# One tile's product of B and u divided between GpSimd and VectorE, and neighbouring products on GpSimd joined

## What is computed

```python
# x is normalised; then the state-space block, with d over 512 inner channels and n over 16 states
xs, res = split(rmsnorm(x) @ W_in)
xs = silu(conv4(xs) + conv_b)
dt, B, C = split(xs @ W_x)                 # 512, 16, 16
dt = softplus(dt @ W_dt)
h = exp(A * dt) * h + dt * B * xs          # for every d and n, step by step in time
y = sum_n(h * C)
out = x + (y * silu(res)) @ W_out          # and a residual around it
# the expert block: 8 chunks of 512 rows, each with weights of its own
h = silu(x @ w1[e]) * (x @ w3[e]);  x + h @ w2[e]
```

## Time and profile before

| | us |
|---|---|
| median of 3 runs (lowest, highest) | 978.1 (977.73, 979.46) |
| the profiled execution | 979.27 |
| its span | 977.5 |
| granted TensorE clock in it | 0.982 |

### The profile page before, as it was taken

How to read it: one execution, slowest core, us unless ns; L and a number is a source line. 1 busy time by engine, 2 the same in 40 slices (tenths; PEclk the granted TensorE clock), 3 DMA queues, 4 the chain that set the end, 5 groups by cost and what they waited for, 6 DMA issues and landing times. The chain is left out here.

```text
span 977.5 us, 13189 instructions
## 1 busy us (share of the span) xinstructions
PE 912.5 (93%) x4204; PEld 601.2 (62%) x4204; DVE 900.1 (92%) x1000; ACT 745.8 (76%) x1356; POOL 893.5 (91%) x425
## 2 busy tenths in 40 slices
PE   6989988999999999999999999999999998677988
PEld 4555455655766566755766567655667557554777
DVE  5889899899999999999999999999999989988983
ACT  4577877888779878888879787888788876567771
POOL 1498899999999999999999999999999999998970
PEclk9998999999999999999999999999999999699999
DMA  5580145011651039111471037310580117401100
GB/s 176 227 295 22 43 164 226 1 68 59 259 202 46 23 114 353 54 68 46 182 293 40 29 102 274 144 68 0 188 331 1 47 60 264 153 22 59 52 1 22
DMA packets 43477, 116.82 MB, mean 120 GB/s; under 512 B 8592, under 2 KB 27024, under 8 KB 34192
## 3 DMA queue, kind: packets, MB, share of 16 engines
q1 hardware_dynamic: 41552, 115.94, 31.9%
q10 hardware_dynamic: 1856, 0.04, 0.1%
HBM read 110.21 MB, written 5.77 MB: 119 GB/s over the span
## 5 line engine op out<-in xcount | busy, mean ns | idle before, releaser
L701 DVE TENSOR_TENSOR_SCAN ring<-ebank,state,ring 128x512 f32<-128x512 f32 (+1 forms) x544 | 626.4, 1203 | 36.8 <-ACT ebank L864 28.7
L553 POOL TENSOR_TENSOR hc<-ring,c_all 128x1024 f32<-128x1024 f32 (+1 forms) x256 | 600.4, 2367 | 18.4 <-DVE ring L701 10.7
L864 ACT ACTIVATE ebank<-dt_,a_neg 128x512 f32<-128x512 f32 (+1 forms) x544 | 353.0, 662 | 143.0 <-DVE ring L701 139.5
L1323 PEld LDWEIGHTS ybank<-ident,hc 128*128 128x128 f32 x1920 | 221.0, 142 | 95.4 <-issue 58.0
L542 POOL TENSOR_TENSOR ring<-b_all,u 128x1024 f32<-128x1024 f32 x110 | 261.1, 2374 | 9.9 <-DVE taken L644 9.5
L1323 PE MATMUL ybank<-ident,hc 128*128 128x128 f32 x1920 | 245.2, 276 | 23.0 <-POOL hc L553 14.3
L681 DVE TENSOR_TENSOR ring<-b_all,ubank 128x1024 f32<-128x1024 f32 x144 | 172.0, 1195 | 0.0
L1248 PE MATMUL gbank<-xT,w 128*128 128x512 f32 x280 | 132.0, 603 | 7.1 <-DVE hb L811 6.8
L1248 PE MATMUL gbank<-xT,w_a 128*128 128x512 f32 x256 | 120.1, 606 | 8.0 <-DVE dt_ L669 4.4
L1248 PE MATMUL gbank<-xs,w_a 128*128 128x512 f32 x224 | 100.8, 593 | 0.7 <-ACT sres L896 0.7
L1248 PEld LDWEIGHTS gbank<-xT,w 128*128 128x128 f32 x280 | 50.2, 192 | 64.0 <-issue 46.0
(11 more groups left out here) (164 smaller groups left out, 854.9 us busy)
## 6 DMA issues: line engine op xcount, KB each, us to landing
b_all<-bc_kept SPq DMA_DIRECT2D x32, 1024.0 KB, 6.7
c_all<-bc_kept SPq DMA_DIRECT2D x32, 1024.0 KB, 8.4
w<-in_L_ffn_w_dram SPq DMA_DIRECT2D x16, 640.0 KB, 4.9
w_a<-in_L_attn_W_in_dram SPq DMA_DIRECT2D x7, 1024.0 KB, 4.8
w_a<-wc_kept SPq DMA_DIRECT2D x7, 1024.0 KB, 4.9
w2s<-in_L_ffn_w_dram SPq DMA_DIRECT2D x8, 640.0 KB, 9.3
xin<-in_L_attn_x_dram SPq DMA_DIRECT2D x9, 512.0 KB, 3.8
x<-in_L_attn_x_dram SPq DMA_DIRECT2D x7, 512.0 KB, 6.4
```

Of the source, the lines that this page charges most:

```text
L553: ch_ok.by(e.tensor_tensor(tile_of(hc, c, q)[:, 0:many, :], tile_of(ring, c, q)[:, 0:many, :], c_all[:, n:n + many, tok], ALU.mult))
L701: h_ok.by(e.tensor_tensor_scan(row, e_of(c, j), row, initial=all_states[:, first:first + 1], op0=ALU.mult, op1=ALU.add))
L864: e_ok.by(e.activation(e_of(c, j), dt_[:, d, tok], ACT.Exp, scale=a_neg[:, d, n0 + n:n0 + n + 1]))
L1323: last = e.matmul(ybank[:, cols(b)], hc[:, q % HC, n, cols(b)], ident[:, :], is_transpose=True, start=(k == 0 and n == 0 and b == 0), stop ...
```

## The change

- `TWO`: in chunks 1 to 6 GpSimd makes the products of B and u for tiles 10 and 11, 17 and 18, 22 and 23 in one instruction each (`bu_two`, 2048 elements), at the place of the first of the two. It waits for what the second's slot needs as well.
- `SHARED`: in those chunks tile 21's product is divided. GpSimd makes state 0 at its old place, VectorE state 1 in a job after tile 20, behind `hidden(0)`, `hidden(1)` and `hidden_tail`. Before tile 21's scans VectorE waits for both.
- u is made for two blocks at once (`u_two`, 1024 elements): blocks 0 and 1 of the next chunk at tile 28, blocks 2 and 3 at tile 2 of the chunk itself. In chunk 0 only the pair at tile 28 is joined.
- On ScalarE `residual(0, 1)` at tile 5 becomes `residual(0)` at tile 4, ahead of `convolved(2)`, and `residual(1)` at tile 5, behind it.

```diff
+    SHARED = 21
+    TWO = (10, 17, 22)
     POOL_BU = (1, 4, 7, 10, 11, 14, 17, 18, 21, 22, 23, 24, 27, 29)
-    DVE_BU = tuple(q for q in range(Q) if q not in POOL_BU)
+    DVE_BU = tuple(q for q in range(Q) if q not in POOL_BU or q == SHARED)
...
         def wait_bu(e, c, q):
             if q in pool_bu(c):
                 bup_ok.wait(e, c, before(pool_bu(c), q) + 1)
-            else:
+            if q in dve_bu(c):
                 bud_ok.wait(e, c, before(dve_bu(c), q) + 1)
...
+        def steady(c):
+            return 0 < c < E - 1
...
+            def u_two(d):
+                def job(c, i):
+                    for k in (d, d + 1):
+                        wait_dt(e, c, k)
+                    xs_ok.wait(e, c)
+                    ub_ok.wait(e, c - 1, d + 2)
+                    e.tensor_tensor(u[:, d:d + 2, :], dt_[:, d:d + 2, :], xs[:, d:d + 2, :], ALU.mult).then_inc(u_ok.sem, 2)
+                return job
...
+                if steady(c) and q == SHARED:
+                    bup_ok.by(e.tensor_tensor(ring[:, q % RING, 0, :], b_all[:, n, :], u[:, d, :], ALU.mult))
+                    return
...
+            def bu_two(c, q):
+                d, n, many, tok = spot(c, q)
+                u_ok.wait(e, c, d + 1)
+                if d == 0:
+                    b_in[n // SG].wait(e, c)
+                    b_in[(n + NG) // SG].wait(e, c)
+                cb, qb = tile_before(c, q + 1, RING)
+                ch_ok.wait(e, cb, qb + 1)
+                st_ok.wait(e, cb, qb // 2 + 1)
+                dst = ring[:, q % RING:q % RING + 2, :, :].rearrange("p a n t -> p (a n) t")
+                e.tensor_tensor(dst, b_all[:, n:n + 2 * NG, :], u[:, d, :].unsqueeze(1).broadcast_to([P, 2 * NG, TC]), ALU.mult
+                                ).then_inc(bup_ok.sem, 2)
...
                 r = q + AHEAD
-                if r < Q and r in pool_bu(c):
+                if steady(c) and r in TWO:
+                    bu_two(c, r)
+                elif r < Q and r in pool_bu(c) and not (steady(c) and r - 1 in TWO):
                     bu(c, r)
...
-            table = [(4, "scan", u_of(ND - 1)), (10, "back", back), (21, "next", front), (24, "front", u_of(0)),
-                     (27, "front", u_of(1)), (29, "front", u_of(2))]
+            table = [(2, "scan", u_two(2)), (10, "back", back), (21, "next", front), (28, "front", u_two(0))]
...
+                if steady(c) and q == SHARED:
+                    bud_ok.by(e.tensor_tensor(ring[:, q % RING, 1, :], b_all[:, n + 1, :], ubank[:, :], ALU.mult))
+                    return
...
-                     (20, "back", hidden_tail), (21, "back", hidden(2)), (22, "back", hidden(3)), (23, "back", hidden(4)),
+                     (20, "back", hidden_tail), (20, "scan", bu_shared), (21, "back", hidden(2)), (22, "back", hidden(3)), (23, "back", hidden(4)),
...
-                     (3, "front", before_conv(3)), (3, "front", convolved(0)), (4, "front", convolved(1)), (5, "front", convolved(2)), (5, "back", residual(0, 1)),
+                     (3, "front", before_conv(3)), (3, "front", convolved(0)), (4, "front", convolved(1)), (4, "back", residual(0)), (5, "front", convolved(2)), (5, "back", residual(1)),
```

More of the change, by code:

```diff
@@ L569, in _ @@
                     bu(0, q)
-            table = [(4, "scan", u_of(ND - 1)), (10, "back", back), (21, "next", front), (24, "front", u_of(0)),
-                     (27, "front", u_of(1)), (29, "front", u_of(2))]
-            table0 = [(3, "late", u_of(1)), (7, "late", u_of(2)), (10, "late", u_of(3)), (23, "next", front),
-                      (27, "front", u_of(0)), (28, "front", u_of(1)), (29, "front", u_of(2))]
-            run(table, table0, [(4, "scan", u_of(ND - 1))], [], group)
+            table = [(2, "scan", u_two(2)), (10, "back", back), (21, "next", front), (28, "front", u_two(0))]
+            table0 = [(3, "late", u_of(1)), (7, "late", u_of(2)), (10, "late", u_of(3)), (23, "next", front), (28, "front", u_two(0))]
+            run(table, table0, [(2, "scan", u_two(2))], [], group)
         @block.vector
@@ L682, in bu, with bu_shared @@
                                           ub.unsqueeze(1).broadcast_to([P, many, tok.stop - tok.start]), ALU.mult))
+            def bu_shared(c, i):
+                if steady(c):
+                    bu(c, SHARED)
             def group(c, q):
@@ L705, in group @@
                     bu(c, q + 2)
-                elif q + 1 < Q and q + 1 in dve_bu(c) and (c, q) != (E - 1, QH + 1):
+                elif q + 1 < Q and q + 1 in dve_bu(c) and (c, q) != (E - 1, QH + 1) and not (steady(c) and q + 1 == SHARED):
                     bu(c, q + 1)
```

## The result

The change makes the kernel slower: 985.85 us (median of 4 runs, 985.32 to 986.53) against 978.06 before, a ratio of 1.0079 with a 95% interval of 1.0064 to 1.0093. Forecast were 983.7 and a range of 977.5 to 988.5. The profiled execution took 986.17, its span 984.4, that is 6.9 more than before. Lines have moved: the scans are L738 (L701 before), the products of c L583 (L553), single products of B and u L559 (L542), joined ones L572, the exponentials L901 (L864), the copies of state L910 (L873), the sum of y L1360 (L1323), the hidden products L848 (L811), the copy of the gate tail L1200 (L1163).

A forecast was written before the change was run, and what follows sets the result against it. The prediction took GpSimd and a ring through TensorE, ScalarE and VectorE to be tied. Six middle chunks x 0.97 = 5.8, less 0.2 in chunk 0, gave +5.6 on the median 978.1: 983.7 us, range 977.5 to 988.5.

The forecast's parts named there:

- The new wait: Joined product of tiles 17 and 18 waits for ScalarE's paired copy of tiles 14 and 15: GpSimd idle 1.9 us.
- the wait before tile 21: VectorE's wait for ScalarE before tile 21, 1.53 us in the kernel before, was to be 0.8 to 0.9.
- the 0.97 a chunk: Tile 17's scan starts 1.25 us later; after ScalarE's slack, silus and tile 21 follow and each middle chunk ends 0.97 later.
- the 0.28 of slack at tile 20: ScalarE's tail-copy wait absorbs part of tile 17's 1.25 us delay; tile 20's second exponential and the silus come 0.95 to 1.0 later.
- What GpSimd sheds: GpSimd's work per middle chunk falls 2.1 us: five joins save 5 x 0.20 = 1.0, half of tile 21 saves 1.09.
- the ring: Cycle through TensorE, ScalarE's tail copy and silus, VectorE's tile 21 and scans, ScalarE's y copy, TensorE; almost without GpSimd, tied with it.
- The residual's halves: First half ahead of ScalarE's third convolution copy removes VectorE's 0.70 us wait at tile 6; VectorE taken 0.75 earlier.
- GpSimd and the ring: GpSimd holds the cycle only before tile 12's sum, so its 2.1 us relief is worth at most some 0.15 a chunk.
- The paying rival: GpSimd was the bound: 2.1 x 6 = 12.6 us gained, 965.5 us, or 972 with half of it; chance 0.11.
- the stall: VectorE waits about 2.0 us at tile 17 for GpSimd's joined product; its scan starts 1.25 us later.
- The half tile on VectorE: VectorE's half of tile 21's product, 0.67 us, falls in its 1.53 wait for ScalarE: no cost, or 0.6 without that cover.
- The reason that the prediction gave: No port contention: scans take 1259 ns (median) both in the first 120 us, with GpSimd partly workless, and in the middle.

The follow-up runs named there:

- copy_alone: The change with all joins kept, but in chunks 1 to 6 ScalarE copies tile 14's last column by itself, a step earlier: 976.64 us, ratio 0.9981.
- join17_only: The kernel before plus only the join of tiles 17 and 18 in chunks 1 to 6: 989.14 us, ratio 1.0108.
- residual_whole: The change with the residual's four row blocks together again at tile 5, behind the third convolution's copy: 989.48 us, ratio 1.0114.
- residual_only: The kernel before plus only the residual's halves at tiles 4 and 5: 977.31 us, ratio 0.9985.
- no_joins: The change with no product of B and u and no u joined; tile 21's division and the residual's halves stay: 977.11 us, ratio 0.9980.
- no_join17: The change without the join of tiles 17 and 18 alone: 975.96 us, ratio 0.9979.
- tile21_whole: The change with tile 21's product whole on GpSimd: 984.49 us, ratio 1.0065.
- no_join17_y26: The change without the join of tiles 17 and 18, and with ScalarE's copy of y of block 2 at tile 26, not 27: 975.52 us, ratio 0.9971.
- the two last kernels: No joins of B and u, tiles 21 and 10 divided, residual's halves, y copy at tile 26: 974.24 us; the second also joins u at tile 28: 975.19.

## Why the prediction was right

- **The new wait**: right in kind and nearly in size. Forecast 1.9 us of idle time, measured 1.87; VectorE's wait "about 2.0", measured 1.99; the joined instruction 4.55, measured 4.54; the wait before tile 21 "0.8 to 0.9", measured 0.89. copy_alone and join17_only show that this alone is the cause. That the idle time came out so close is in part luck: GpSimd was done with tile 14 0.34 earlier than before (51.61 for 51.95 from the chunk's first scan) and not 0.6, which shortens it by 0.26, and the copy came and was taken up 0.21 later, which lengthens it.
- **The term that was mis-sized** is the 0.97 a chunk, which measured 1.17. Tile 17 was put 1.25 late and was 1.41. The residual's halves gave 0.66, not the 0.75 that I took, and GpSimd started 0.17 behind the copy's end, where 0.05 was taken. From there on the 0.28 of slack at tile 20 was as forecast (tile 19 was 1.44 late, tile 21 1.17). Six chunks x 1.17 = 7.0; chunk 0, from which 0.2 was taken off, is 0.09 shorter in the profile of the change; and the span grew by 6.9. The medians differ by 7.8, interval 6.3 to 9.1, where 5.6 was forecast.
- **What GpSimd sheds** was put too high: 2.1 a chunk, measured 1.75. The sum took means of single instructions, but one of GpSimd's instructions starts some 0.05 before the record of the last one ends. Back to back, starts in chunk 3 are 1.24 (512 elements), 2.32 (1024) and 4.49 (2048) apart. By these a join saves 0.15 and not 0.20, five of them and the half tile 5 x 0.15 + 1.08 = 1.8. It did not matter to the time, since hardly any of it was on the ring.
- **The residual's halves**: right; their absence costs the change 0.65 a chunk (residual_whole). Missed was that ScalarE's earlier copies of the gate products free TensorE's two waits of 0.1 for their banks (in the kernel before two gate matmuls start 0.52 and 0.53 behind the last one, in residual_only 0.43). That is 0.2 a chunk, nearly all of it what the halves give by themselves (0.16).
- **GpSimd and the ring**: the size held (at most 0.15 a chunk from GpSimd, measured 0.13 from no_joins to no_join17). The account of it did not: I let the ring run by TensorE all the way from the input product and put GpSimd beside it, and two expectations built on that failed. Runs showed two chains of nearly one length that join at tile 12's sum. That nobody is seen waiting for GpSimd for over 0.15 us did not mean that it had time to spare.
- **The paying rival** fell: without the stall all that is left of the change shortens a chunk by 0.30, a ratio of 0.9979. The Trainium skill's advice to take the engine of highest occupancy first (Perfetto Trace Analysis, Identifying the Most-Contended Engine) would have led astray in this kernel, where three engines are within 4 us of the period of 112.5.
- **The half tile on VectorE**: no cost, as forecast. Its 0.69 lay in the wait. In all six chunks it ran beside the joined product of tiles 22 and 23, which took 4.54 (4.535 to 4.548) and takes the same 4.54 in tile21_whole, without the half tile. So the shared port of which the Trainium skill warns (Perfetto Trace Analysis, Optimizing Scalar/DVE Operations) does not show in this pair. The reason that the prediction gave was read wrongly off: between 35 and 120 us GpSimd is busy for 73.5 of 85, so those scans are no sample without it. In the kernel before only three scans of 512 columns find GpSimd at rest, at 35.0, 36.9 and 85.2; they take 1.285, 1.285 and 1.259, no less than the median of 1.259.

## What to carry to other kernels

Joining two instructions moves the second one forward, and with it every wait that it has: before a join, list for each semaphore who raises it, behind what, and when, and compare that with the first one's place. Here a copy done for two tiles at once made the parity of the joined pair decide (10 with 11 and 22 with 23 were ready, 17 with 18 not). And where several engines are near the period, look for the chains between the engines, not for the busiest: work taken from one pays only between the points where that engine's chain is joined by another.

## What the runs showed of the hardware

- **A join on GpSimd saves less than its start.** The 2048-element product takes 4.541 us by its record where two of 1024 take 4.74; from start to start it is 4.49 against 2 x 2.32, so 0.15 is saved. But the joined one needs the slot of the tile whose product of c stands right before it, and so waits for its own engine: 0.23 of idle time, where two instructions without such a wait follow each other with no gap, the second even starting 0.05 before the first one's record ends. From the start of tile 7's product of c to that of tile 9's it is 9.42 in the change (409.75 to 419.17) and 9.28 in the kernel before (407.76 to 417.04): the join costs 0.14.
- **Chunk 0 comes in two lengths, and which one does not go by its code.** It lasted 118.6 in six profiles (copy_alone, join17_only, tile21_whole, residual_only, residual_whole, no_join17_y26) and 119.5 to 119.9 in the other eight (before, the change, no_join17 among them); chunk 0 has the same lists in tile21_whole and in the change. The granted TensorE clock between 40 and 80 us is 0.96 in the six and 0.91 in the eight. In each TensorE waits 4.4 for VectorE's dt until about 73, and around that the clock is at the lower of its two levels (1.2 GHz): in tile21_whole between 73.4 and 76.7, in no_join17 from 72.4 to 79.2. That this sets the length is not shown. Medians a microsecond apart are no verdict then; the chunks' own length is a better one, as chunks 2 to 6 of a profile agree to 0.05 us or better (0.08 in the two last kernels). The two rows are of tile21_whole and of no_join17:

```profile
40.00:80.00 40.00, 34.60 (x145) 21.89 (x144) 35.57 (x33) 27.85 (x51) 38.40 (x18) 0.96 0.72 271
```

```profile
40.00:80.00 40.00, 35.53 (x147) 22.90 (x145) 35.98 (x32) 26.48 (x48) 38.35 (x18) 0.91 0.72 275
```
